# Row attention: softmax sums from the exponentials' accumulator, two rows weighed together, denominators inverted on VectorE

## The reference

```python
q = split_heads(q_x @ Wq) / math.sqrt(C_HID)        # q_x: the group-normed x
k = split_heads(kv_x @ Wk)
v = split_heads(kv_x @ Wv)
a = jnp.einsum('bnhqc,bnhkc->bnhqk', q, k)
a = a + mask_bias + tri_bias
a = jax.nn.softmax(a, axis=-1)
o = jnp.einsum('bnhqk,bnhkc->bnhqc', a, v)
o = jnp.swapaxes(o, -2, -3)
g = jax.nn.sigmoid(q_x @ Wg).reshape(lead + (H, C_HID))
o = o * g
o = o.reshape(lead + (H * C_HID,))
return o @ Wo                                        # and x is added to it
```

## Time and profile before

| | |
|---|---|
| median of 3 runs | 4797.06 us (4793.52 to 4877.1) |
| the profiled execution, its own time | 4796.05 us |
| its span, first to last instruction | 4793.8 us |
| busy over the span | PE 92%, DVE 72%, ACT 58%, POOL 55% |
| granted TensorE clock over the span | 0.958 |
| attention stage | from about 112 to 1985 us of the span |
| one row of the image in the steady part | 7.23 us |

### The profile page before, as it was taken

The page is one execution under the profiler, slowest core; times in us unless marked ns, Lnnn a source line. Parts: engine busy times, 40 slices in busy tenths (PEclk is TensorE's granted clock), DMA queues, the critical chain, the costliest instruction groups (busy, mean ns, idle before and its releaser), DMA issues. The chain is left out here.

```text
span 4793.8 us, 108030 instructions
## 1 busy us (share of the span) xinstructions
PE 4411.2 (92%) x36006; PEld 3297.2 (69%) x36006; DVE 3431.3 (72%) x10053; ACT 2804.1 (58%) x6302; POOL 2614.8 (55%) x2043
## 2 busy tenths in 40 slices
PE   5999999999999999777899989999749997999996
PEld 5777777777777777534577766777424445999995
DVE  7888888888888888651566666666429995567666
ACT  0888888888888888402333343333325662666665
POOL 0999999999999999402233322333105551122222
PEclk8999999999999999887999999999869998999997
DMA  7222222222222222597322222222567887999995
GB/s 311 63 77 73 75 74 74 75 74 76 75 75 75 73 75 74 187 381 248 104 71 73 71 84 71 73 71 73 223 220 214 277 278 245 264 292 293 291 291 137
DMA packets 803939, 713.02 MB, mean 149 GB/s; under 512 B 60693, under 2 KB 700948, under 8 KB 794839
## 3 DMA queue, kind: packets, MB, share of 16 engines
q1 hardware_dynamic: 784875, 672.74, 45.8%
q10 hardware_dynamic: 14717, 20.01, 1.2%
q0 software_dynamic: 3808, 13.47, 0.7%
HBM read 506.70 MB, written 199.29 MB: 147 GB/s over the span
## 5 line engine op out<-in xcount | busy, mean ns | idle before, releaser
L309 POOL TENSOR_TENSOR at_bias<-at_tri,at_mask 128x1024 f32<-128x1024 f32 x512 | 1216.0, 2375 | 27.9 <-DMA at_mask<-in_L_conv_mask_bias_dram 12.1
L427 ACT ACTIVATE at_probs<-at_neg_s,at_neg_max 128x256 f32<-128x256 f32 x2048 | 871.4, 505 | 0.7 <-DVE at_neg_max L478 0.7
L478 DVE CUSTOM_DVE_ANT_0 at_neg_s<-at_p_s,at_bias 128x256 f32<-128x256 f32 x2048 | 759.8, 418 | 7.6 <-PE at_p_s L350 2.9
L301 POOL TENSOR_TENSOR at_paired_t<-at_probs_t 128x512 f32<-128x512 f32 x512 | 655.9, 1281 | 9.7 <-ACT at_probs_t L419 5.6
L361 PE MATMUL at_p_t<-all_ident,at_probs 128*128 128x128 f32 x4096 | 628.3, 276 | 0.6 <-DVE at_probs_t L486 0.4
L969 ACT ACTIVATE ml_h<-ml_p_turns,l_b 128x512 f32<-128x512 f32 x384 | 263.8, 687 | 607.2 <-PE ml_p_turns L928 607.2
L361 PEld LDWEIGHTS at_p_t<-all_ident,at_probs 128*128 128x128 f32 x4096 | 476.0, 141 | 131.7 <-issue 104.1
L1070 POOL TENSOR_TENSOR ml_x2t<-ml_z,ml_xb 128x512 f32<-128x512 f32 x128 | 163.7, 1279 | 675.1 <-DVE ml_z L1036 675.1
L937 PEld LDWEIGHTS ml_p<-l_w1s,ml_h 128*128 128x128 f32 x4096 | 471.9, 192 | 52.7 <-issue 52.7
L1990 POOL TENSOR_TENSOR dw_room<-dw_room,all_b_plain 128x512 f32<-128x512 f32 x128 | 176.9, 1382 | 589.1 <-DMA dw_room<-x3t 589.1
L928 PE MATMUL ml_p_turns<-ml_h,l_w 128*128 128x512 f32 x1024 | 485.3, 597 | 2.3 <-DVE ml_h L1002 2.3
(11 more groups left out here) (230 smaller groups left out, 9110.2 us busy)
## 6 DMA issues: line engine op xcount, KB each, us to landing
dw_xw<-planes SPq DMA_DIRECT2D x128, 528.0 KB, 4.7
sp_xs<-x SPq DMA_DIRECT2D x128, 512.0 KB, 9.1
dw_wts<-patch_w SPq DMA_DIRECT2D x128, 512.0 KB, 6.2
planes<-pw_plane SPq DMA_DIRECT2D x128, 264.0 KB, 3.2
in_xs<-in_x_dram SPq DMA_DIRECT2D x32, 1024.0 KB, 7.7
at_xs<-in_x_dram SPq DMA_DIRECT2D x256, 128.0 KB, 2.5
at_kvs<-in_L_conv_kv_x_dram SPq DMA_DIRECT2D x256, 128.0 KB, 2.7
at_mask<-in_L_conv_mask_bias_dram SPq DMA_DIRECT2D x256, 128.0 KB, 3.3
```

Of the source, the lines that this page charges most:

```text
L301: pool.tensor_tensor(paired_t[:, n % 2, part], probs_t[:, n % 3, part, 0], probs_t[:, n % 3, part, 1], ALU.add).then_inc(paired, 1)
L309: pool.tensor_tensor(bias[:, n % 2, part], tri[:, part], mask[:, n % 4].unsqueeze(1).broadcast_to((128, 4, COLS)), ALU.add).then_inc(maske ...
L427: e = act.activation(probs[:, h, qh, :], neg_s[:, n % 2, h, qh, :], ACT.Exp, bias=neg_max[:, n % 2, i:i + 1], scale=-1.0)
L478: t = dve.tensor_tensor_reduce(neg_s[:, n % 2, h, qh, :], p_s[h][:, qh, :], bias[:, n % 2, i, :], -1.0, 3.0e38, ALU.add, ALU.min, neg_max[ ...
```

## The change

The row sums no longer come from a matmul. Each exponential also writes out its accumulator (`sums`). POOL copies the 8 sums of a row over 32 channels each (`spread_sums`, tile `spread`), between the two halves of `add_mask`, in place of the two `pair` additions. PE turns the `spread` of two rows (`turn_sums`) into `p_t[0]`, the tile of the even heads. DVE makes the denominators of the two rows from it in one instruction of 512 columns, and inverts them with one RECIPROCAL of 512 columns. ACT's logarithm and exponential are gone. `weigh`, `project_out`, `denominator`, `gate`, `residual` and the store take two rows at once (a pair q holds rows 2q and 2q+1): turn_sums(q) stands in the even step 2q+2, denominator, weigh, invert and gate in the odd step 2q+3, project_out and residual in the even step 2q+4, and the store in step 2q+5. The rings of `xs` and `kvs` grow from 8 to 10 rows, `vs` and `gate_e` from 4 to 6, `probs_t` from 3 to 4.

```diff
-            def pair(n, half):
-                pool.wait_ge(even_read, 2 * n + half + 1)
-                pool.wait_ge(odd_read, 2 * n + half + 1)
...
+            def spread_sums(n):
+                pool.wait_ge(exped, (n + 1) * HEADS)
+                if n >= 4:
+                    pool.wait_ge(sums_turned, (n - 4) // 2 + 1)
+                pool.tensor_copy(spread[:, n % 4], sums[:, n % 4].unsqueeze(3).broadcast_to((128, HALVES, HEADS, HEAD_DIM))
+                                 ).then_inc(sums_spread, 1)
...
             for n in range(-2, rows + 2):
-                for half in range(2):
-                    if exists(n - 1):
-                        pair(n - 1, half)
-                    if exists(n + 2):
-                        add_mask(n + 2, half)
+                if exists(n + 2):
+                    add_mask(n + 2, 0)
+                if exists(n - 1):
+                    spread_sums(n - 1)
+                if exists(n + 2):
+                    add_mask(n + 2, 1)
...
+                if h == 0 and n >= 3:
+                    pe.wait_ge(den_made, (n - 1) // 2)
...
+            def turn_sums(q):
+                pe.wait_ge(sums_spread, 2 * q + 2)
+                pe.wait_ge(even_read, min(4 * q + 6, 2 * rows))
+                for r in range(2):
+                    for half in range(HALVES):
+                        mm = pe.transpose(p_t[0][:, r, half * 128:(half + 1) * 128],
+                                          spread[:, (2 * q + r) % 4, half].rearrange("p h d -> p (h d)"), ident[:, :])
+                mm.then_inc(sums_turned, 1)
+
+            def weigh(q):
+                pe.wait_ge(even_read, 4 * q + 4)
+                pe.wait_ge(odd_read, 4 * q + 4)
+                pe.wait_ge(vg_read, 2 * q + 2)
+                if q >= 1:
+                    pe.wait_ge(x1_made, q)
+                for r in range(2):
+                    n = 2 * q + r
+                    for kh in range(HALVES):
+                        for h in range(HEADS):
+                            ch = slice(HEAD_DIM * h, HEAD_DIM * (h + 1))
+                            mm = pe.matmul(p_out[ch, r, :], vs[:, n % 6, kh, ch], probs_t[:, n % 4, h, kh, :],
+                                           start=kh == 0, stop=kh == HALVES - 1)
                 mm.then_inc(weighed, 1)
...
-                for h in range(HEADS):
-                    mm = pe.matmul(p_out[HEAD_DIM * h:HEAD_DIM * (h + 1), 1, :], ones[:, :], paired_t[:, n % 2, h, :],
-                                   start=True, stop=True)
...
                     e = act.activation(probs[:, h, qh, :], neg_s[:, n % 2, h, qh, :], ACT.Exp,
-                                       bias=neg_max[:, n % 2, i:i + 1], scale=-1.0)
+                                       bias=neg_max[:, n % 2, i:i + 1], scale=-1.0,
+                                       accum_out=sums[:, n % 4, qh, h:h + 1])
...
-            def invert(n):
-                act.wait_ge(den_made, n + 1)
-                act.activation(den[:, n % 2], den[:, n % 2], ACT.Ln).then_inc(den_step, 1)
-                act.wait_ge(den_step, 2 * n + 1)
-                act.activation(den[:, n % 2], den[:, n % 2], ACT.Exp, scale=-1.0).then_inc(den_step, 1)
...
+            def denominator(q):
+                dve.wait_ge(sums_turned, q + 1)
+                dve.wait_ge(vg_read, 2 * q + 2)
+                if q >= 2:
+                    dve.wait_ge(gated, q - 1)
+                dve.scalar_tensor_tensor(out=den[:, q % 2], in0=gate_e[:, 2 * q % 6:2 * q % 6 + 2], scalar=1.0, in1=p_t[0][:, :, :],
                                          op0=ALU.add, op1=ALU.mult).then_inc(den_made, 1)
...
+            def invert(q):
+                dve.wait_ge(den_made, q + 1)
+                dve.reciprocal(den[:, q % 2], den[:, q % 2]).then_inc(inverted, 1)
```

More of the change, by code:

```diff
@@ L256, in exists, with pair_at @@
             return 0 <= n < rows
+        def pair_at(n, lag):
+            return (n - lag) // 2 if n % 2 == lag % 2 and lag <= n < rows + lag else None
         @block.sync
@@ L278, in _ @@
                 load_mask(n)
-            for n in range(-2, rows + 2):
+            for n in range(-2, rows + 5):
                 if n + 4 < rows:
@@ L380, in project_out @@
-            def project_out(n):
-                pe.wait_ge(gated, n + 1)
-                for half in range(HALVES):
-                    mm = pe.matmul(p_out[:, 0, half * 128:(half + 1) * 128], og[:, n % 2, half * 128:(half + 1) * 128], wo_s,
-                                   start=True, stop=True)
+            def turn_sums(q):
[6 more added lines that the diff above has]
+                mm.then_inc(sums_turned, 1)
@@ L385, in project_out @@
+            def project_out(q):
+                pe.wait_ge(gated, q + 1)
+                for r in range(2):
+                    for half in range(HALVES):
+                        mm = pe.matmul(p_out[:, r, half * 128:(half + 1) * 128],
+                                       og[:, q % 2, r, half * 128:(half + 1) * 128], wo_s, start=True, stop=True)
                 mm.then_inc(out_made, 1)
             pe.wait_ge(const_loaded, 16 * 6)
-            pe.wait_ge(cleared, 1)
-            for n in range(-2, rows + 2):
+            for n in range(-2, rows + 3):
@@ L405, in _ @@
                     turn_probs(n, 2)
-                if exists(n - 2):
-                    project_out(n - 2)
+                q = pair_at(n, 4)
+                if q is not None:
+                    project_out(q)
                 if exists(n):
                     turn_probs(n, 3)
+                q = pair_at(n, 2)
+                if q is not None:
+                    turn_sums(q)
         @block.scalar
@@ L512, in read_turn @@
                 dve.tensor_copy(kvt[:, :], p_in[:, 1, :]).then_inc(turn_read, 1)
-            for n in range(-2, rows + 2):
-                if exists(n - 2):
-                    denominator(n - 2)
+            for n in range(-2, rows + 3):
+                weighing, leaving = pair_at(n, 3), pair_at(n, 4)
+                if weighing is not None:
+                    denominator(weighing)
                 if exists(n):
@@ L520, in _ @@
                     read_turn(n + 2)
-                if exists(n - 2):
-                    gate(n - 2)
+                if weighing is not None:
+                    invert(weighing)
+                    gate(weighing)
                 if exists(n + 1):
```

140 lines of the change are left out of this document (63 added, 77 removed).

## The result

The changed kernel takes 5645.0 us (median of 4 runs, 5638.33 to 5726.03) against 4795.29 us of the kernel before in the same comparison: 1.176 times as long, 95% interval 1.175 to 1.178. The highest of the four, like the 4877.1 us among those of the kernel before, is an execution in a slower state that both kernels show, some 80 us longer; the ratio leaves it out. The profiled execution has a span of 5639.7 us. Slower was forecast, 5390 us with a range to 5520; the loss was 850 us in place of 594.

A forecast was written before the change was run, and what follows sets the result against it. PE and POOL were taken to bound the kernel at 7.23 us a row. Ring 15.77 + reciprocal 3.2 + accumulators 0.15 = 19.12 us a pair, 596 us more over 256 rows: 5390 us; own range 5300 to 5510, 8 in 10 5030 to 5520.

The forecast's parts named there:

- The wait that the change adds: At turn_sums on PE: it needs DVE's even-head read, 1.5 us late there, which closes a ring of waits.
- The ring: Five pieces of PE and DVE waiting on each other in turn: 15.77 us + R for two rows, against 14.46.
- pieces 1, 2: Ring: 1, PE from even to odd read, 3.93 us; 2, DVE odd step, 4.77 + R; 5, residual to even read, 1.99.
- The prices: Costs of new instructions: RECIPROCAL 3.2 us, accumulator output 0.1 us each, POOL's copy at most 0.64 us.
- the third rival: The ring does not close and PE's own 6.84 us a row decides: faster, 4696 us; chance 0.05.
- pieces 3 and 4: PE's ring pieces: 3, turn_probs(even, 0) to scores, 1.50 us; 4, even step from scores to residual, 3.58 us.
- R: Time of DVE's RECIPROCAL of 512 columns: 3.2 us, with ends 0.6 and 4.3 us.
- the second rival: RECIPROCAL dearer (4.3 us, above 5500 us) or PE's clock falls (each 5% adds 56 us); chance 0.09.
- Both engines stand at the pace: PE and POOL both at the kernel's 7.23 us a row, so relieving both looks like a gain.
- Even a reciprocal for nothing makes it longer: With R at nothing the ring's 15.77 us for two rows still exceeds the 14.46 us they took.
- The cheap reciprocal: First rival: RECIPROCAL as fast as a copy, R = 0.6 us, ACT's way decides, 5044 to 5085 us; chance 0.23.
- The estimate by eight passes for each column: Iterative divide on DVE read as eight passes per column: R of 4.3 us, kernel at 5530 us.

The follow-up runs named there:

- e1: The changed kernel with DVE's RECIPROCAL issued right behind the denominator, in front of the odd row's read_probs: 5148.35 us, ratio 1.074.
- e2: The changed kernel with the inversion back on ACT as a logarithm and an exponential of 512 columns: 5147.54 us, ratio 1.073.
- e4: The changed kernel with the projection of values and gate done three times in each even step, same result: 5459.51 us, ratio 1.137.
- e10: The kernel before with POOL's pair additions cut to half of the queries from row 2 on: 4797.5 us, ratio 1.000.
- e11: The changed kernel with turn_sums in the odd step, ACT's logarithm and exponential and DVE's gate in the even step: 5022.52 us, ratio 1.047.
- e12: The changed kernel with the projection of values and gate done twice in each even step, same result: 5561.34 us, ratio 1.159.
- e5: The changed kernel with turn_sums in the odd step and inversion on ACT behind the first head's exponentials of the odd step: 5126.15 us, ratio 1.068.
- the unpaired ones: Two kernels with accumulator row sums turned per row, inversion on ACT, otherwise the kernel before; the second has transposes before weigh: 4749.07 and 4744.54 us.

## Why the prediction was right in its mechanism and wrong in its size

**The wait that the change adds** was right. PE waits 1.72 us in front of turn_sums for the read of the even head (1.5 worked out), DVE 2.64 us in front of the odd row's read (over 2). The ring exists, and its pieces 1, 2 (with the RECIPROCAL as measured) and 5 as read above are within 0.21 us of the forecast. Taking the reciprocal out of the ring (e1, e2) gives back 497 us, the clock's part included.

**The prices** were right. RECIPROCAL 3.34 us (3.2 forecast from one-column rows), accumulator 0.09 us a piece (0.1), POOL's copy 0.40 us (at most 0.64). One slip had no effect on the forecast: the sum of PE's work takes off 0.13 us for the switch that the text puts at 0.1 at most, which moves the third rival by 4 us.

**The step that failed** is the length of the ring's pieces 3 and 4. They were taken from the earlier trace rows, where PE never waits and the clock is 1.00, and the forecast kept that clock: "the ring is 15.77 us + R". The clock stood only with the second rival, for 5% steps of 56 us, beside the remark that PE would wait over a quarter of the time; that holds at the forecast's own R too, and in the sum the fall was put at nothing. The runs show that behind the wait of 3.4 us the granted clock falls in every pair of the five that repeat, to 0.57 over 7 us in one and to 0.76 to 0.81 in the others, and pieces 3 and 4 take 6.76 us on their mean in place of 5.03. e4 fills the wait: at the full clock its two pieces take 5.26 us, and 186 us go. These 186 us, with some 60 us by which e4's ring of 19.6 us is longer than the 19.12 us forecast, make up nearly all of the 255 us between 5390 and 5645. By the rival's steps the stage's clock of 0.90 would have been 112 us. The term was mis-sized by leaving out a mechanism that the text itself named.

**"Both engines stand at the pace"** was half wrong. e10 shows that POOL was not a bound. It carried nothing in the sum, but it was a reason to hope in the third rival.

**"Even a reciprocal for nothing makes it longer"** was right in sign: e2 with 17.2 us a pair, e11 with 16.2. The forecast did not say why in full. I put all of it on the wait at turn_sums; e11, without that wait and at full clock, keeps 227 us of the loss. What the rest is stays open. One candidate is the unevenness of steps that take two rows' work in one and none in the other, while every cover in the order was cut for equal steps; the other is the gate's wait for ACT, behind which add_bias stands in e11.

**The other rivals.** The cheap reciprocal fell with the first row of the profile. Its price of 5044 to 5085 us is 60 to 105 us under e1 and e2, which are the nearest thing to it that was run. The estimate by eight passes for each column, 4.3 us, was too high: the trace shows 3.34 us, 6.5 ns a column. The other reading, 0.6 us, was far too low.

## What to carry to other kernels

When an order written by hand has no slack on the bound engine, look at what a new instruction waits for and at how long ago that was ready, before counting its cost: turn_sums costs 0.44 us and waits 1.7. Put a long instruction where its engine is idle; three instructions earlier it was worth 497 us here. Where a change makes TensorE wait for microseconds, price what follows at both levels of the clock, and check the granted clock by window. Of the kernels run here the unpaired ones were the fastest; whether equal steps are the reason was not isolated.

## What the runs showed of the hardware

- RECIPROCAL on VectorE took 3342 ns for 512 columns of fp32 and 1743 ns for 256: 6.2 ns for each further column, where a copy takes 1.05.
- An accumulator read on ScalarE has a row of 196 ns and lengthens the spacing of exponentials of 256 columns by 0.09 us, from 0.40 to 0.49. On VectorE the spacing with an accumulator read, 0.345 us, was that of an instruction without one, 0.34 us.
- The same wait of TensorE was followed by the lower clock in some pairs and not in others: 2.5 us in e12 and 1.5 us in e5. The longest wait by itself does not tell: e4 waits 1.66 and 1.72 us in each pair and keeps 1.00, while e5, which waits 1.53 us and at most 0.3 us elsewhere, has 0.96 in the stage.
- A kernel became faster by work added to TensorE, 186 us in e4 and 84 us in e12, which no sum of durations would give.
